# A token table beside the row buffers: when a mixture-of-experts kernel may load a row buffer anew

## The chip, the cores and the metric

The kernel runs on one core of a Trainium2 chip. The metric is the device time of one execution in microseconds (us); less is better. Quoted times are medians over several executions of one kernel. The profile is of one further execution.

## The reference

The reference is one transformer layer on 2048 tokens of 128 floats, in float32. First comes layer norm and a 16-head linear attention (cosformer) with its residual. Then comes layer norm and a mixture of experts (MoE) with its residual, which is the part that matters here:

```python
logits = xf @ gate_w                                   # 2048 x 8 experts
top_w, top_idx = jax.lax.top_k(logits, 2)
top_w = softmax(top_w)
h = gelu(einsum('td,edf->tef', xf, w1) + b1)           # 128 -> 512
y = einsum('tef,efd->ted', h, w2) + b2                 # 512 -> 128
out = einsum('ted,te->td', y, combine)                 # weights of the two chosen experts
```

## The kernel before

**Attention.** The tokens go through in four super-chunks of 512 (NS = 4). Each super-chunk's layer norm, gate logits, two best experts and row places are worked out while the next one's attention runs; the last one is handled in two halves (units 3 and 4).

**Sorting by expert.** For each token and each of its two experts GpSimd writes a row to `ybuf` in HBM with an indirect DMA (`rows_out`, L473). A row has 144 floats: the 128 normalised values, then the token's number in column D (as an unsigned integer; it names the row of `zbuf` to which the result goes), then the expert's weight in column D + 1. `ybuf` thus holds, expert by expert, blocks of 128 rows. NB = 39 blocks are computed; a table `tab` says for each block its expert and its place. The first 17 blocks (`FIRST[1]`) are listed before the last super-chunk has been sorted, the other 22 after a second table.

**A block's life.** For block b the steps are, engine by engine:

- SyncE, `load_block(b)`: reads the place from `tab`, issues the DMA of the block's 128 rows into row buffer `yb[b % 10]` (L376, 72 KB), and the DMA of the expert's first weights into `w1b[b % 6]` (L379, 256 KB). It runs ahead of the compute as far as the rings allow. Before the second DMA it waits until TensorE is through with block b - 6 (`h_ps`, L378). Before the first one, from block 10 on, it waits for `z_out` of block b - 10 (L373), that is, until that block's results have landed in HBM.
- TensorE, in the order written out in `step(b)`: transposes block b + 2 (`block_rows`, L1324), multiplies block b + 1 by w1 (`hidden`, L1337), multiplies block b by w2 (`down`, L1352). A transposition waits for the rows of its block (`yb_in`) and for `xb_ok`, the copy of the block before.
- ScalarE, `hidden(b)`: four activations (Gelu with bias, L638).
- VectorE: `block_rows(b)` loads the expert's number, copies the bias (L970) and copies the transposed block out of PSUM (L981); `weighed(b)` adds b2 (L986), and multiplies by the weight in column D + 1 of the row buffer (L990), which raises `z_ok`. In its order `block_rows(b + 3)` follows `weighed(b)`, and `weighed(b + 1)` follows that.
- GpSimd, `results_out(b)`: an indirect DMA (L511) scatters the 128 result rows to `zbuf`. Its offsets are read from column D of the row buffer, so the row buffer is in use until then. The order is by hand: `RESULTS_AT` says which blocks are scattered once `z_ok` has come to 3, 4, 8, 9, ... 14, since GpSimd also has late `rows_out` to issue (`LATE_ROWS_AT`); from block 14 on each block is scattered once it is weighed.

`z` has eight buffers (ZR), the row buffers are ten (YR), w1's are six (WR). At the end SyncE and ScalarE wait for all scatters, load `zbuf`, VectorE adds it to the residual, and the output is stored.

In the trace the 39 blocks can be counted along a line: the first row of L990 is block 0; the first row of L1324 is block 2 and the first of L981 too (blocks 0 and 1 are turned and copied at L1252 and L976).

Of the kernel before, what the change touches and what calls it, by code (L numbers as in the profile page):

```python
# [25 lines left out]
U32 = mybir.dt.uint32  # L26
I32 = mybir.dt.int32

P = 128
T, D = 2048, 128  # L30
# [47 lines left out]
NB = (2 * T + E * (TB - 1)) // TB  # L78
# [19 lines left out]
YR, ZR, WR, XR = 10, 8, 6, 4  # L98

def moe_block(nc, x, Wq, bq, Wk, bk, Wv, bv, Wo, bo, gate_w, w1, b1, w2, b2,
              c_rot, c_pair, c_ident, c_small, c_tri, c_ids, out, ybuf, zbuf):
    with ExitStack() as ctx:
        def sb(name, shape, dt=F32):
            return ctx.enter_context(nc.sbuf_tensor(name, shape, dt))

        def sem(name):
            return ctx.enter_context(nc.semaphore(name))
# [66 lines left out]
        yb = [sb(f"yb{k}", [P, ROW]) for k in range(3)]  # L175
        w1b = [sb(f"w1b{k}", [P, F]) for k in range(2)]
        b1_all = sb("b1_all", [P, E, FB])
        b2_all = sb("b2_all", [P, E, D])
        b1t = sb("b1t", [P, XR, FB])
        zs = sb("zs", [P, 2, D])  # L180
        xb = sb("xb", [P, XR, P])
        acc = x_sb
# [33 lines left out]
        z_out = [sem(f"z_out{k}") for k in range(ZR)]  # L216
# [92 lines left out]
        z_ok = sem("z_ok")  # L309
# [8 lines left out]
        def _(sp):  # L318
# [52 lines left out]
            def load_block(b):  # L371

                if b >= YR:  # L373
                    sp.wait_ge(z_out[(b - YR) % ZR], 16 * ((b - YR) // ZR + 1))
                at = sp.value_load(tab[0:1, 1, b:b + 1], min_val=0, max_val=PLACES)
                sp.dma_start(yb[b % YR][:], ybuf[bass.ds(at, TB), :]).then_inc(yb_in[b % YR], 16)  # L376
                if b >= WR:
                    sp.wait_ge(h_ps, 2 * (b - WR) + 2)  # L378
                sp.dma_start(w1b[b % WR][:], w1[bass.ds(at // PITCH, 1), :, :].rearrange("e p n -> p (e n)")  # L379
                             ).then_inc(w1_in[b % WR], 16)  # L380
# [4 lines left out]
            for u in range(TABLES[0] + 1):  # L385
                unit_landed(u)
            sp.wait_ge(tab_ok, 1)
            load_block(0)
            load_block(1)
            sp.wait_ge(sc_ps, NS * PAIRS)  # L390
            for b in range(2, FIRST[1]):
                load_block(b)
# [16 lines left out]
        def _(pool):  # L409
# [98 lines left out]
            def results_out(b):  # L508
                if b >= PACED:
                    pool.wait_ge(z_ok, b + 1)  # L510
                pool.indirect_dma_start(zbuf, bass.IndirectOffsetOnAxis(ap=yb[b % YR][:, D:D + 1].bitcast(U32), axis=0),  # L511
                                        z[:, b % ZR, :], None, bounds_check=2 * T - 1, oob_is_err=False).then_inc(z_out[b % ZR], 16)

            for i in range(NS):
# [5 lines left out]
            for k in range(1, PACED + 1):  # L520
                pool.wait_ge(z_ok, k)
                for u, m in LATE_ROWS_AT.get(k, ()):
                    rows_out(u, m)
                for b in RESULTS_AT.get(k, ()):
                    results_out(b)
                if k == 2:
                    second_rows(NS)
            for b in range(PACED, NB):
                results_out(b)
# [135 lines left out]
        def _(dve):  # L665
# [291 lines left out]
            def row_of(all_experts, expert):  # L957
                return all_experts[:, bass.ds(expert, 1), :].rearrange("p e n -> p (e n)")

            def expert_of(b):  # L960

                if b == 0:
                    dve.wait_ge(tab_ok, 1)
                    dve.wait_ge(b_in, 32)
                if b == FIRST[1]:
                    dve.wait_ge(tab_ok, 2)
                which[b] = dve.value_load(tab[0:1, 0, b:b + 1], min_val=0, max_val=E - 1)
                if b >= XR:
                    dve.wait_ge(h_ok, (b - XR + 1) * FB)
                dve.tensor_copy(b1t[:, b % XR, :], row_of(b1_all, which[b]))  # L970

            def first_rows():
                expert_of(0)
                expert_of(1)
                dve.wait_ge(xT_ps, NS + 1)
                dve.tensor_copy(xb[:, 0:2, :], ps[:, 6, 0:2 * P].rearrange("p (b r) -> p b r", b=2)).then_inc(xb_ok, 2)  # L976

            def block_rows(b):
                expert_of(b)
                dve.wait_ge(xb_ps, b - 1)  # L980
                dve.tensor_copy(xb[:, b % XR, :], ps[:, 5, b % 2 * P:b % 2 * P + P]).then_inc(xb_ok, 1)  # L981

            def weighed(b):

                dve.wait_ge(z_ps, b + 1)
                dve.tensor_tensor(zs[:, b % 2, :], ps[:, z_bank(b), 0:D], row_of(b2_all, which[b]), ALU.add).then_inc(zs_ok, 1)  # L986
                if b >= ZR:
                    dve.wait_ge(z_out[b % ZR], 16 * (b // ZR))
                dve.wait_ge(zs_ok, b + 1)
                dve.tensor_scalar(z[:, b % ZR, :], zs[:, b % 2, :], yb[b % YR][:, D + 1:D + 2], None, ALU.mult  # L990
                                  ).then_inc(z_ok, 1)

            def add_results(k):
# [5 lines left out]
                dve.tensor_tensor(tile, tile, zin[:, 1, k * SC:(k + 1) * SC, :], ALU.add).then_inc(out_ok, 1)  # L999

            first_rows()
            taken(NS - 1, GROUPS - 2)
            taken(NS - 1, GROUPS - 1)
            residual(NS - 1, SC - 2)
            best_two(NS - 1, 5)
            block_rows(2)
            norm2_stats(NS)
            norm2(NS)
            places(NS - 1)
            shares(NS - 1)  # L1010
            weighed(0)
            normed2(NS)
            block_rows(3)
            weighed(1)
            block_rows(4)
            weighed(2)
            block_rows(5)
# [438 lines left out]
```

## Time and profile before

| | |
|---|---|
| median of 3 executions | 378.92 us (378.6 to 380.24) |
| the profiled execution, first to last instruction | 389.7 us; no other time is given for it |
| TensorE busy | 358.1 us, 92% |
| VectorE, ScalarE, GpSimd busy | 62%, 40%, 33% |
| MoE blocks in the trace | about 266 us (first row load) to 374 us (last scatter issued) |

The span is that of the execution under the profiler and lies 10.8 us above the median of the runs without it. Busy is the time in which an engine has an instruction running. A row of a timeline gives start, duration, engine, line and operation, what is written and read, a count where instructions of a kind are merged, and in brackets how long the engine was idle before and what ended that. The duration of a DMA-issuing row (SPq) is that of the issue and not of the transfer.

### The profile page before, as it was taken

Reading aid. Unit: us, or ns where it says so; the run is one execution under the profiler, and the core shown is the slowest. Engines: PE = TensorE matmul, PEld = TensorE weight load, DVE = VectorE, ACT = ScalarE, POOL = GpSimd, SP = SyncE. Lnnn points to the kernel's source line nnn. Section 1 sums busy time; section 2 is a strip of 40 time slices with the busy share of each in tenths; the row PEclk is TensorE's granted clock in tenths of the full one; section 3 lists DMA queues with packets and bytes.
Section 4 is the critical chain, followed back from the end, with each engine's and each line's share of the span. In section 5 each row is a group of like instructions: output and inputs, shape, how many; then the busy total and the mean of one; then the engine's idle time right before and its main releaser. Section 6 shows DMA issues by size and latency. Waiting matters only on the chain.

```text
span 389.7 us, 10955 instructions
## 1 busy us (share of the span) xinstructions
PE 358.1 (92%) x4125; PEld 323.4 (83%) x4125; DVE 241.4 (62%) x735; ACT 156.7 (40%) x369; POOL 129.8 (33%) x130
## 2 busy tenths in 40 slices
PE   8999999999999999999999999999978887999910
PEld 7777999888988988898998889898978777999910
DVE  4889664778756477875647787766545424444415
ACT  3773322565122256512225651222443434555500
POOL 4022511121285112028511302443265454444420
PEclk9999999999999999999999999999998989999985
DMA  7932432330001000000100007004625256876229
GB/s 252 332 156 84 177 130 96 156 129 2 16 31 33 16 2 1 0 19 31 41 8 3 0 14 219 24 19 115 179 93 144 81 166 179 234 203 188 63 81 248
DMA packets 32771, 38.64 MB, mean 99 GB/s; under 512 B 4139, under 2 KB 25024, under 8 KB 31696
## 3 DMA queue, kind: packets, MB, share of 16 engines
q1 hardware_dynamic: 27248, 31.90, 26.4%
q0 software_dynamic: 2272, 4.46, 3.3%
q10 hardware_dynamic: 3200, 1.58, 1.5%
q8 instruction: 34, 0.56, 0.6%
q14 instruction: 17, 0.14, 0.1%
HBM read 22.91 MB, written 15.47 MB: 98 GB/s over the span
## 4 chain that ended last, share of the span: by engine, by line
PE 79%; DVE 7%; DMA 4%; issue 4%; POOL 2%; another core or an unknown queue 1%; ACT 1%; DVEq 1%; SPq 1%; ACTq 0%; POOLq 0%
PE ps L1166 8%; PE ps L1352 8%; PE ps L1128 8%; PE ps L1173 7%; PE ps L1337 7%; PE ps L1145 7%; PE ps L1202 7%; PE ps L1047 5%; PE ps L1049 5%; PE ps L1048 5%; PE ps L1193 4%; PE ps L1092 3%; DMA zin<-zbuf 2%; PE ps L1297 2%; PE ps L1324 1%
## 5 line engine op out<-in xcount | busy, mean ns | idle before, releaser
L597 ACT ACTIVATE os<-ps 128x260 f32<-128x260 f32 x64 | 24.8, 388 | 103.4 <-PE ps L1173 103.3
L638 ACT ACTIVATE hT<-ps,b1t 128x128 f32<-128x128 f32 x156 | 44.9, 368 | 47.9 <-PE ps L1337 26.7
L473 POOL DMA_INDIRECT ybuf<-yr,slot x32 | 31.8, 994 | 75.3 <-DVE yr L845 32.8
L431 POOL TENSOR_TENSOR on<-tcs,rden 128x1024 f32<-128x1024 f32 x16 | 30.4, 1901 | 64.4 <-DVE rden L773 64.4
L511 POOL DMA_INDIRECT zbuf<-z,yb x39 | 37.9, 972 | 39.0 <-DVE z L990 22.3
L760 DVE TENSOR_TENSOR state<-ps,state 128x260 f32<-128x260 f32 x64 | 27.3, 427 | 35.5 <-ACT os L597 29.3
L1352 PE MATMUL ps<-w_sb,hT 128*128 x312 | 43.4, 284 | 3.5 <-DVE zs L986 3.3
L750 DVE TENSOR_TENSOR am<-ps,pair 128x1024 f32<-128x1024 f32 x32 | 38.7, 1208 | 10.0 <-issue 7.5
L1337 PE MATMUL ps<-xb,w1b 128*128 128x128 f32 x312 | 43.9, 286 | 0.0
L1352 PEld LDWEIGHTS ps<-w_sb,hT 128*128 128x128 f32 x312 | 39.3, 198 | 4.3 <-issue 4.2
L1166 PE MATMUL ps<-vcs,am 128*64 128x65 f32 x1024 | 42.5, 225 | 0.2 <-issue 0.2
L1166 PEld LDWEIGHTS ps<-vcs,am 128*64 128x64 f32 x1024 | 36.8, 137 | 3.9
L1337 PEld LDWEIGHTS ps<-xb,w1b 128*128 128x128 f32 x312 | 39.7, 199 | 0.0
L1173 PE MATMUL ps<-vcs,kn 128*64 128x130 f32 x512 | 39.6, 275 | 0.0
L1128 PE MATMUL ps<-qT,kT 64*128 64x128 f32 x512 | 38.0, 285 | 1.0 <-DVE am L750 0.9
L1128 PEld LDWEIGHTS ps<-qT,kT 64*128 64x128 f32 x512 | 31.7, 187 | 7.3 <-issue 6.6
L1145 PE MATMUL ps<-state,qT 64*128 64x130 f32 x480 | 34.8, 279 | 0.5 <-DVE tcs L766 0.4
L715 DVE TENSOR_SCALAR vcs<-os,cs 128x512 f32<-128x512 f32 x64 | 32.6, 551 | 1.1
L1145 PEld LDWEIGHTS ps<-state,qT 64*128 64x128 f32 x480 | 30.2, 187 | 2.5 <-DVE tcs L766 1.4
L1202 PE MATMUL ps<-wo_sb,oT 128*128 128x128 f32 x256 | 31.6, 278 | 0.0
L1202 PEld LDWEIGHTS ps<-wo_sb,oT 128*128 128x128 f32 x256 | 29.8, 192 | 1.7 <-issue 1.4
L711 DVE TENSOR_TENSOR os<-ps,bv_all 128x512 f32<-128x512 f32 x32 | 22.0, 689 | 14.7 <-PE ps L1049 14.7
(120 smaller groups left out, 585.7 us busy)
## 6 DMA issues: line engine op xcount, KB each, us to landing
w1b<-in_L_ffn_w SPq DMA_DIRECT2D x39, 256.0 KB
ybuf<-blank SPq DMA_DIRECT2D x8, 1152.0 KB, 4.7
yb<-ybuf SPq DMA_DIRECT2D x39, 72.0 KB
w_sb<-in_L_ffn_w SPq DMA_DIRECT2D x8, 256.0 KB
x_sb<-in_L_attn_x SPq DMA_DIRECT2D x4, 256.0 KB, 5.4
pair<-c_pair SPq DMA_DIRECT2D x16, 64.0 KB, 2.4
zin<-zbuf SPq DMA_DIRECT2D x4, 256.0 KB, 5.5
zin<-zbuf ACTq DMA_DIRECT2D x4, 256.0 KB, 6.0
```

The source lines that it names most:

```text
L473: pool.indirect_dma_start(ybuf, bass.IndirectOffsetOnAxis(ap=slot[:, k, c:c + 1], axis=0), yr[:, k, c, :], None).then_inc(y_out[u], 16)
L511: pool.indirect_dma_start(zbuf, bass.IndirectOffsetOnAxis(ap=yb[b % YR][:, D:D + 1].bitcast(U32), axis=0), z[:, b % ZR, :], None, bounds_c ...
L638: act.activation(hT[:, b % 2, f, :], ps[:, b % 2 * 2 + f // 2, f % 2 * P:f % 2 * P + P], ACT.Gelu, bias=b1t[:, b % XR, f:f + 1]).then_inc( ...
L715: last = dve.tensor_scalar(vcs[:, m // 2, (m % 2) * 8:(m % 2) * 8 + 8, s, 0:DH], vb[:, m % 2, :].rearrange("p (h d) -> p h d", d=DH), cs4[ ...
L750: dve.tensor_tensor(am[:, p % 2, :, :, :], ps[:, 0:2, :].rearrange("p r (q t) -> p r q t", t=P), pair[:, c, None, None, :].broadcast_to([P ...
L1128: last = mm(ps[:, r, b * P:(b + 1) * P], kT[rows, of, c * P:(c + 1) * P], qT[rows, of, c * P:(c + 1) * P], start=True, stop=True)
L1145: mm(ps[:, 2 + 2 * (n % 2) + r, 0:2 * CS].rearrange("p (s b v) -> p b s v", s=2, b=2)[:, q, :, :], qT[rows, 2 * g + q, c * P:(c + 1) * P], ...
L1166: mm(ps[t:t + 64, 2 + 2 * (n % 2) + r, q * VW:q * VW + VW], am[:, n // 2 % 2, r, (2 * g + q) % (PH // 2), t:t + 64], vcs[:, c, g * GH + 2 ...
L1173: last = mm(ps[64 * r:64 * r + 64, 2 + 2 * (n % 2) + q, 2 * CS:3 * CS], kn[:, c, (2 * g + q) * P + r * DH:(2 * g + q) * P + (r + 1) * DH], ...
L1202: last = mm(ps[:, 7, at:at + D], oT[:, c % 2, pr, :], wo_sb[:, pr, :], start=(pr == 0), stop=(pr == NP - 1))
L1337: last = mm(ps[:, b % 2 * 2 + f // 2, f % 2 * P:f % 2 * P + P], w1b[b % WR][:, f * P:(f + 1) * P], xb[:, b % XR, :], start=True, stop=True ...
L1352: last = mm(ps[:, z_bank(b), 0:D], hT[:, b % 2, f, :], w, start=(f == 0), stop=(f == FB - 1))
```

## The change

A table `tokens` of 128 x 39 integers is added. In `block_rows(b)`, after the copy of the transposed block, VectorE copies column D of the row buffer to column b of the table; for blocks 0 and 1 it does so ahead of their common copy in `first_rows`. The scatter of block b reads its offsets from the table. `load_block(b)` now waits, from block 10 on, until block b - 10 is weighed (`z_ok`) and no longer until its scatter has landed.

```diff
+        tokens = sb("tokens", [P, NB], U32)
...
             def load_block(b):
 
                 if b >= YR:
-                    sp.wait_ge(z_out[(b - YR) % ZR], 16 * ((b - YR) // ZR + 1))
+                    sp.wait_ge(z_ok, b - YR + 1)
...
             def results_out(b):
                 if b >= PACED:
                     pool.wait_ge(z_ok, b + 1)
-                pool.indirect_dma_start(zbuf, bass.IndirectOffsetOnAxis(ap=yb[b % YR][:, D:D + 1].bitcast(U32), axis=0),
+                pool.indirect_dma_start(zbuf, bass.IndirectOffsetOnAxis(ap=tokens[:, b:b + 1], axis=0),
                                         z[:, b % ZR, :], None, bounds_check=2 * T - 1, oob_is_err=False).then_inc(z_out[b % ZR], 16)
...
+            def tokens_of(b):
+                dve.tensor_copy(tokens[:, b:b + 1], yb[b % YR][:, D:D + 1].bitcast(U32))
+
             def first_rows():
                 expert_of(0)
                 expert_of(1)
                 dve.wait_ge(xT_ps, NS + 1)
+                tokens_of(0)
+                tokens_of(1)
                 dve.tensor_copy(xb[:, 0:2, :], ps[:, 6, 0:2 * P].rearrange("p (b r) -> p b r", b=2)).then_inc(xb_ok, 2)
 
             def block_rows(b):
                 expert_of(b)
                 dve.wait_ge(xb_ps, b - 1)
                 dve.tensor_copy(xb[:, b % XR, :], ps[:, 5, b % 2 * P:b % 2 * P + P]).then_inc(xb_ok, 1)
+                tokens_of(b)
```

## Rows read from the trace of the kernel before

**Rows 1.** Busy time, granted clock and DMA share in three stretches of the MoE.

```profile
core 0: us, PE busy (x) PEld busy (x) DVE busy (x) ACT busy (x) POOL busy (x), PEclk, DMA share, GB/s
286.00:304.00 18.00, 14.27 (x108) 13.54 (x108) 7.99 (x45) 7.07 (x25) 9.83 (x12) 0.91 0.39 116
304.00:330.00 26.00, 20.63 (x161) 19.82 (x160) 9.12 (x40) 10.39 (x36) 12.64 (x13) 0.93 0.52 150
330.00:368.00 38.00, 37.94 (x326) 37.06 (x325) 17.94 (x76) 21.74 (x77) 18.43 (x19) 1.00 0.64 179
```

**Rows 2.** Waits of TensorE from 303 to 370 us, the only row.

```profile
PE ps L1324 <- DVE xb L981: 5.4, 4, 1.9
```

**Rows 3.** Waits in SyncE's queue after 255 us: in total, times, longest.

```profile
SPq L375 <- DMA zbuf<-z,yb: 3.3, 5, 1.2
SPq L379 <- PE ps L1337: 3.2, 2, 2.4
```

**Rows 4.** SyncE's loads: block 9's weights, blocks 10, 12, 13.

```profile
287.95 0.33 SPq L379 DMA_DIRECT2D w1b<-in_L_ffn_w  x1
294.56 0.33 SPq L376 DMA_DIRECT2D yb<-ybuf  x1
...
296.79 0.33 SPq L379 DMA_DIRECT2D w1b<-in_L_ffn_w  x1
299.58 0.01 SPq L376 DMA_DIRECT2D yb<-ybuf  x1
...
308.18 0.51 SPq L376 DMA_DIRECT2D yb<-ybuf  x1
308.74 0.71 SPq L379 DMA_DIRECT2D w1b<-in_L_ffn_w  x1
```

**Rows 5.** TensorE around the transposition of block 13 (311.38).

```profile
307.68 0.30 PE L1324 MATMUL ps<-ident,yb 128*128 128x128 f32 x1
...
311.38 0.30 PE L1324 MATMUL ps<-ident,yb 128*128 128x128 f32 x1 [1.40 <-DVE xb L981]
...
313.36 0.27 PE L1324 MATMUL ps<-ident,yb 128*128 128x128 f32 x1
```

**Rows 6.** VectorE: block 7 weighed, then block 9, and the copy of 12.

```profile
304.10 0.29 DVE L990 TENSOR_SCALAR z<-zs,yb 128x128 f32<-128x128 f32 x1
...
309.69 0.29 DVE L986 TENSOR_TENSOR zs<-ps,b_all 128x128 f32<-128x128 f32 x1 [2.17 <-remote]
...
310.94 0.29 DVE L981 COPY xb<-ps 128x128 f32<-128x128 f32 x1
```

**Rows 7.** GpSimd's scatters, two of a burst of three, and the next.

```profile
306.47 0.98 POOL L511 DMA_INDIRECT zbuf<-z,yb  x1 [0.30 <-issue]
307.75 0.97 POOL L511 DMA_INDIRECT zbuf<-z,yb  x1 [0.31 <-issue]
311.15 0.97 POOL L511 DMA_INDIRECT zbuf<-z,yb  x1 [2.43 <-DVE z L990]
```

**Rows 8.** DMA issues by kind on the page: KB, median us from issue to landing.

```profile
pair<-c_pair SPq DMA_DIRECT2D x16, 64.0 KB, 2.4
zin<-zbuf SPq DMA_DIRECT2D x4, 256.0 KB, 5.5
```

**Rows 9.** All engines in the steady part: block 22 weighed, blocks 26 and 27 turned.

```profile
341.63 0.29 DVE L990 TENSOR_SCALAR z<-zs,yb 128x128 f32<-128x128 f32 x1
...
343.00 0.27 PE L1324 MATMUL ps<-ident,yb 128*128 128x128 f32 x1
...
344.98 0.30 PE L1324 MATMUL ps<-ident,yb 128*128 128x128 f32 x1
```

**Rows 10.** VectorE by form from 330 to 370 us.

```profile
L986 DVE TENSOR_TENSOR zs<-ps,b_all 128x128 f32<-128x128 f32 x20 | 5.8, 291 | 9.4 <-issue 6.9 <-PE ps L1352 2.6
L970 DVE COPY b1t<-b_all 128x4 f32 x20 | 3.4, 170 | 9.4 <-ACT hT L638 8.6 <-issue 0.8
```

**Rows 11.** All z and L511 instructions: duration in ns, least, median, most.

```profile
L990 DVE TENSOR_SCALAR z<-zs,yb x39: 285/286/565, 283.6 to 372.8; 128x128 f32<-128x128 f32 x39
L511 POOL DMA_INDIRECT zbuf<-z,yb x39: 969/970/998, 291.6 to 373.9; - x39
```

**Rows 12.** VectorE's last copy of a block, near the end.

```profile
368.50 0.28 DVE L981 COPY xb<-ps 128x128 f32<-128x128 f32 x1
```

**Rows 13.** The common copy of blocks 0 and 1, and TensorE's first `hidden`.

```profile
270.64 0.42 DVE L976 COPY xb<-ps 128x256 f32<-128x256 f32 x1
...
275.33 1.06 PE L1337 MATMUL ps<-xb,w1b 128*128 128x128 f32 x8
```

## The prediction

> **What bounds the kernel now.** I read the stretches first, then who waits, then single timelines. From 330 to 368 us TensorE is busy 37.94 of 38 us at full clock [rows 1]: a block costs 1.98 us there (343.00 to 344.98, [rows 9]), and nothing that arrives earlier can shorten it. From 304 to 330 us it is busy only 20.63 of 26 us, and from 286 to 304 us 14.27 of 18 us [rows 1]. Those 5.4 and 3.7 us are the only places where a change in load order can gain, so the question is what these gaps wait for.
>
> TensorE's waits name VectorE's copy of the block before (5.4 us, four times) and no DMA at all [rows 2]. The transposition of block 13 shows it. It starts at 311.38, right after the copy of block 12 at 310.94 + 0.29 = 311.23 [rows 5, 6]. That copy is late because `weighed(9)` began only at 309.69 after 2.17 us of idleness, released by something the profile can't name ("remote", [rows 6]). In the same time GpSimd issues scatters back to back, at 306.47 and 307.75, with 0.3 us between them [rows 7], and VectorE goes on some 1.9 us after the last of a burst has started. The later gaps have the same look: a burst of three scatters, then VectorE's late row. So what I see is a chain from GpSimd's bursts to late signals to VectorE to TensorE. The change leaves the order of the scatters, `RESULTS_AT`, as it is.
>
> **What the removed wait costs today.** SyncE does stand still. Block 9's weights are issued at 287.95 and block 10's rows at 294.56; block 12's rows go at 299.58, block 13's at 308.18 [rows 4]. Block 13 needs the landing of block 3's scatter, which by `RESULTS_AT` isn't issued until block 7 is weighed. The row of waits at that line books 3.3 us in five waits [rows 3], much less than the 8.6 us from 299.58 to 308.18; it keeps only what it can match, so I go by the timeline.
>
> Does it reach TensorE? A load of 64 KB by SyncE lands in 2.4 us [rows 8]; the 72 KB of block 13 then land at 308.18 + 2.4 = 310.6, and TensorE turned the block at 311.38. Slack 0.8 us. The weights, issued at 308.74, are used 2.1 us after that, about 313.5. The trace has no landing time for them; the bounds are 2.4 us as for 64 KB and 5.5 us as for 256 KB from HBM [rows 8], giving 311.1 to 314.2. The row that names TensorE's waits has no DMA [rows 2], so I take them as in time. In this profiled execution the removed wait is thus hidden behind the late copy, and taking it away alone is worth 0.
>
> **The same without the profiler.** The profiled span, 389.7 us, is 10.8 us over the median of 378.92. The gaps of the MoE sum to 5.4 + 3.7 = 9.1 us, of the same size, so I reckon that part of them does not exist in a timed run. Then the loads have less cover. In the steady part a block is turned 5.3 us after the weighing of the block six before it (block 22 is weighed at 341.63, block 27 turned at 344.98, block 28 hence at 344.98 + 1.98 = 346.96, [rows 9]). Block 7 is weighed at 304.10 [rows 6], so an undisturbed TensorE would turn block 13 at 309.4, while its rows land at 310.6. The delay is 1.1 us. It is paid once: block 14 follows by SyncE's pace of one load in 1.7 us (block 13's rows at 308.18, and its weights 0.56 later, then 1.1 us to the next), faster than TensorE's 1.98. So the gain lies between 0 (all gaps are real in timed runs) and 1.1 us (none is). I take the middle, 0.5 us: 378.9 - 0.5 = 378.4.
>
> **What the loads do instead.** After the change SyncE is held by `h_ps` alone, the wait for block b - 6 at the weights. Block 12's rows could go at 296.79 + 1.1 = 297.9, block 13's 1.7 us later at 299.6, some 8.6 us earlier than now. Behind the new wait on `z_ok` the same things queue as before (place, rows, weights), and `z_ok` is raised before the scatter is issued, so the wait can never end later than the old one. From block 17 on loads also need the second table and the late rows, which have not changed; the order can gain up to 8 us of lead and no more, and in the steady part the lead is of no use [rows 1]. The same bytes move, a part of them from the 304 to 330 stretch (DMA share 0.52) to the one before (0.39) [rows 1]. There they meet the late rows of units 3 and 4. I cost that at 0.
>
> **The added copies.** There are 39 copies of 128x1. None is in the trace; the nearest row is the 128x4 copy from SBUF to SBUF, 170 ns, 20 of them [rows 10]. The lower bound is the pace of overlapped rows, near 0.1 us; the upper one is 0.17 us of VectorE each, 6.6 us in all. They stand between the copy of a block and L986 of an earlier block, and ahead of L986 VectorE idles 9.4 us in 20 blocks, 0.47 us each [rows 10]. That covers 0.17 us with 0.3 us to spare, so they cost 0. In the stage with gaps they stand before an idle time of some 2 us [rows 6]. The two in `first_rows` stand in front of the common copy of blocks 0 and 1 at 270.64; TensorE's first use of it is at 275.33, 4.3 us after its end [rows 13]. No copy stands behind the last block's: VectorE's last one starts at 368.50 [rows 12], and the three scatters that end the stage follow later. Were the cover gone, 39 x 0.17 = 6.6 us would be the price.
>
> The scatter's offsets come from another place in SBUF, the same 128 numbers; L511 keeps its 970 ns [rows 11].
>
> A rule speaks against such copies. L511 takes 969 to 998 ns in all 39 cases although L990, SBUF to SBUF too, runs beside some of them [rows 11]; only L990 itself is sometimes long, up to 565 ns. The Trainium skill (SBUF — State Buffer, "SBUF: two separate sides") says that VectorE in a mode using two ports and GpSimd lock each other out of a shared port for a whole instruction, and that fp32 copies within SBUF hold up GpSimd's descriptor writing. By that rule each copy would delay a scatter by its own length, 0.17 us, off the path, or wait for one. The trace agrees only in so far as L990 is at times long.
>
> **The rivals.**
>
> *A, more than 1.1 us is gained (0.16).* Weights too may be late today: at 5.5 us they land at 314.2, against an undisturbed need at 309.4 + 2.1 = 311.5, which is 2.7 us. Or the gaps themselves come from the crowd of catching-up loads and scatters in 304 to 330, and go when loads are spread: half of the 5.4 us gives 2.7 as well. Time 378.9 - 2.7 = 376.2. For it: the gaps end at 330, about when SyncE has caught up. Against: TensorE waits for no DMA [rows 2], and at 286 to 304 there are gaps of the same look while SyncE is standing still [rows 1, 4].
>
> *B, slower: copies outgrow their cover (0.07).* A copy that has to wait for GpSimd to finish a scatter (970 ns, [rows 11]) may take as long as the worst L990 beyond its usual, 565 - 286 = 279 ns, on top of its 170: 450 ns against 470 of cover. With the full 970 ns before it a copy takes 1.14 us, 0.67 beyond cover; of the 20 blocks in the filled stretch half may meet a scatter: 0.67 x 10 = 6.7 us, 385.6 at worst. At half that strength it is 3.3 us, 382.2. It decides from 0.47 us of copy on. Against it: L970, the same kind of copy, has a mean of 170 ns in the same stretch [rows 10].
>
> *C, nothing at all (within the forecast, but 0.0 us).* All gaps are real without a profiler: 378.9.
>
> A fourth, that earlier loads crowd out the late rows and delay the second table's blocks (0.05), bites where a late row lands after block 16's load is issued and holds the queue at block 17; I put it at one landing of 64 KB less the lead that the blocks have now, 2.4 - 0.8 = 1.6 us [rows 8], 380.5.
>
> **How the numbers follow.** The forecast with C holds 0.72, and the range of this case alone is 377.6 to 379.6 with the scatter of the timed runs. A has 0.16, B 0.07, the fourth 0.05. A change under 0.5%, 1.9 us, can't be told from none here; the bounds are 377.0 and 380.8. Faster: A, and a little of the forecast's low end, 0.19. Slower: B and a bit of the fourth, 0.09. The range reaches to A's 376.2 and stops at 380.3, short of B.
>
> **What would show it.** Right: SyncE's rows of block 13 go out near 300 instead of 308.18; TensorE's gaps between 286 and 330 stay, with VectorE's "remote" idleness after scatter bursts, and from 330 on a block costs 1.98 us; the new copy takes 0.1 to 0.2 us, and the idleness ahead of L986 shrinks by about that. Wrong: TensorE's busy time in the stretch from 304 to 330 rises well above 20.63 us (A), or idle TensorE appears after 330 with VectorE named as releaser (B). A timed gain above 2 us with an unchanged pattern of gaps would mean that the loads mattered in a way that this profile hides.

## The result, and the profile after

| | before | changed |
|---|---|---|
| median | 379.85 us (8 runs, 378.6 to 380.4 but for one of 406.98) | 376.93 us (375.08 to 378.09, 8 runs) |
| ratio, 95% interval | | 0.9921, 0.9898 to 0.9943 |
| profiled execution: span, own time | 389.7 us, not known | 375.2 us, 377.03 us |

The change saves 0.8% of 379.85, about 3.0 us (2.2 to 3.9 by the interval); the execution of 406.98 us counts as slow and is left out of the ratio. The forecast was 378.4 us, with 376.2 to 380.3 as its range. The time lies inside the range but below what the likeliest case allowed (377.6), and the chance given to a gain over 0.5% was 0.19.

After the change a profiled execution's own time is known: it is its span plus 1.8 us (377.03 - 375.2). So a profile doesn't stretch this kernel, and the first profile of the kernel before, 10.8 us above the median, was of an odd execution; why it was slow isn't known. A new profile of the same program (experiment e1) has a span of 377.7 us and a time of 379.58. Both sides are read from these two from here on. The columns are those of [rows 1].

The kernel before, profiled anew:

```profile
286.00:304.00 18.00, 16.92 (x142) 15.80 (x141) 9.83 (x47) 9.20 (x32) 11.88 (x14) 1.00 0.46 128
304.00:330.00 26.00, 24.50 (x204) 23.45 (x204) 11.40 (x48) 13.59 (x48) 13.55 (x15) 1.00 0.76 220
```

The changed kernel:

```profile
286.00:304.00 18.00, 17.01 (x146) 16.29 (x144) 10.61 (x60) 9.35 (x34) 12.07 (x14) 1.00 0.68 195
304.00:330.00 26.00, 25.68 (x214) 24.67 (x213) 12.69 (x63) 13.81 (x49) 14.76 (x16) 1.00 0.70 199
```

Of the 9.1 us of gaps in [rows 1] only 1.1 + 1.5 = 2.6 us are in a usual execution of the old kernel, at full clock throughout; after the change 1.0 + 0.3 = 1.3 are left. The waits say which went. From 284 to 356 us, in total, times, longest; first the old kernel, then the changed one:

```profile
PE ps L1324 <- DMA yb<-ybuf: 1.5, 2, 1.1
PE ps L1324 <- DVE xb L981: 0.9, 2, 0.7
```

```profile
PE ps L1331 <- DVE xb L987: 0.9, 2, 0.6
PE ps L1359 <- DVE zs L993: 0.2, 1, 0.2
```

The first row is new beside [rows 2]: TensorE did wait for row buffers. The timeline of the old kernel shows where. SyncE issues the rows of blocks 12, 13, 14 and 15:

```profile
292.85 0.33 SPq L376 DMA_DIRECT2D yb<-ybuf  x1
...
299.94 0.33 SPq L376 DMA_DIRECT2D yb<-ybuf  x1
...
301.75 0.33 SPq L376 DMA_DIRECT2D yb<-ybuf  x1
...
303.41 0.33 SPq L376 DMA_DIRECT2D yb<-ybuf  x1
```

TensorE turns blocks 13, 14, 15 and 16:

```profile
301.86 0.33 PE L1324 MATMUL ps<-ident,yb 128*128 128x128 f32 x1
...
305.12 0.33 PE L1324 MATMUL ps<-ident,yb 128*128 128x128 f32 x1 [1.15 <-DMA yb<-ybuf]
...
307.75 0.33 PE L1324 MATMUL ps<-ident,yb 128*128 128x128 f32 x1 [0.34 <-DMA yb<-ybuf]
...
309.71 0.27 PE L1324 MATMUL ps<-ident,yb 128*128 128x128 f32 x1
```

Block 13 is turned 1.92 us after its rows were issued (299.94 to 301.86), with no wait booked, so these rows landed within 1.92 us. Block 14's took 3.37 us from issue to transposition and block 15's 4.34, and TensorE stood waiting for both. In the four other profiles with the old wait and ten buffers (e2, e5, e6, e11, below) it is the same: block 13 is turned 1.86 to 1.91 us after its issue, block 14 only 2.8 to 3.2 us after, with a booked wait of 0.6 to 1.0 us. After the change the same four transpositions of blocks 13 to 16 follow at a pace of 2.0 to 2.1 us with nothing in brackets, and the rows of block 13 were issued at 291.48, 10.6 us ahead:

```profile
302.12 0.27 PE L1331 MATMUL ps<-ident,yb 128*128 128x128 f32 x1
...
304.11 0.30 PE L1331 MATMUL ps<-ident,yb 128*128 128x128 f32 x1
...
306.25 0.27 PE L1331 MATMUL ps<-ident,yb 128*128 128x128 f32 x1
...
308.24 0.30 PE L1331 MATMUL ps<-ident,yb 128*128 128x128 f32 x1
```

The second place is the end, where nothing was expected. The page's rows of the final load, KB each and median us to landing; old kernel, then the changed one:

```profile
zin<-zbuf SPq DMA_DIRECT2D x4, 256.0 KB, 5.6
zin<-zbuf ACTq DMA_DIRECT2D x4, 256.0 KB, 6.1
```

```profile
zin<-zbuf SPq DMA_DIRECT2D x4, 256.0 KB, 4.8
zin<-zbuf ACTq DMA_DIRECT2D x4, 256.0 KB, 5.3
```

The last scatter is issued at 361.81 in the one and at 360.49 in the other, so from there to the end it is 377.7 - 361.81 = 15.9 us and 375.2 - 360.49 = 14.7 us:

```profile
361.81 0.97 POOL L511 DMA_INDIRECT zbuf<-z,yb  x1 [0.31 <-issue]
```

```profile
360.49 0.97 POOL L512 DMA_INDIRECT zbuf<-z,tokens  x1 [0.34 <-issue]
```

In the chain of work that ended last (start, duration), the scatter's landing takes 2.08 us in both, and the final load differs by 1.19 us:

```profile
361.81 2.08 DMA zbuf<-z,yb
365.66 7.90 DMA zin<-zbuf
```

```profile
360.49 2.08 DMA zbuf<-z,tokens
364.35 6.71 DMA zin<-zbuf
```

The two spans differ by 2.5 us. From the transposition of block 12 to that of block 18 it is 14.3 us (299.43 to 313.74) against 12.7 (300.00 to 312.66), which is 1.65; the end gives 1.2; the rest, 0.35 us the other way, is spread over the other stretches. So there are two terms, a known one that was sized too small, and one that the forecast didn't have.

The added copy is within what was costed (durations as minimum, median and maximum in ns). The scatters have the median of e1, 972 ns; their longest is 1027 ns against 1003 in e1:

```profile
L974 DVE COPY tokens<-yb x39: 140/144/154, 267.1 to 355.4; 128x1 uint32<-128x1 uint32 x39
L512 POOL DMA_INDIRECT zbuf<-z,tokens x39: 970/972/1027, 286.7 to 360.5; - x39
```

### The profile page after: what moved, and what is told of

Same layout as the page of the kernel before. It is cut to its first block, busy times and chain, and to the rows that moved or that the text cites. A ratio compares the mean times of both kernels' runs of the same rounds, so it can differ in the third digit from the quotient of the medians.

```text
span 375.2 us, 10993 instructions
## 1 busy us (share of the span) xinstructions
PE 351.7 (94%) x4125; PEld 319.0 (85%) x4125; DVE 244.9 (65%) x774; ACT 156.5 (42%) x369; POOL 130.1 (35%) x130
## 4 chain that ended last, share of the span: by engine, by line
PE 82%; DVE 5%; DMA 5%; issue 3%; POOL 1%; ACT 1%; SPq 1%; ACTq 0%; DVEq 0%; POOLq 0%
PE ps L1135 9%; PE ps L1173 9%; PE ps L1359 8%; PE ps L1344 8%; PE ps L1152 7%; PE ps L1180 7%; PE ps L1209 7%; PE ps L1054 6%; PE ps L1056 5%; PE ps L1055 5%; PE ps L1200 4%; PE ps L1099 3%; DMA zin<-zbuf 2%; PE ps L1331 1%; DMA ident<-c_ident 1%
## 5 line engine op out<-in xcount | busy, mean ns | idle before, releaser
L512 POOL DMA_INDIRECT zbuf<-z,tokens x39 | 38.0, 975 | 31.1 <-DVE z L997 25.6
L1344 PE MATMUL ps<-xb,w1b 128*128 128x128 f32 x312 | 42.3, 278 | 0.0
L1359 PEld LDWEIGHTS ps<-w_sb,hT 128*128 128x128 f32 x312 | 37.8, 191 | 1.9 <-issue 1.4
L1135 PE MATMUL ps<-qT,kT 64*128 64x128 f32 x512 | 37.2, 284 | 1.0 <-DVE am L751 0.9
L1344 PEld LDWEIGHTS ps<-xb,w1b 128*128 128x128 f32 x312 | 37.9, 192 | 0.0
L1152 PE MATMUL ps<-state,qT 64*128 64x130 f32 x480 | 33.3, 277 | 0.0
```

Of the source, the lines that this page charges most:

```text
L512: pool.indirect_dma_start(zbuf, bass.IndirectOffsetOnAxis(ap=tokens[:, b:b + 1], axis=0), z[:, b % ZR, :], None, bounds_check=2 * T - 1, o ...
L1135: last = mm(ps[:, r, b * P:(b + 1) * P], kT[rows, of, c * P:(c + 1) * P], qT[rows, of, c * P:(c + 1) * P], start=True, stop=True)
L1152: mm(ps[:, 2 + 2 * (n % 2) + r, 0:2 * CS].rearrange("p (s b v) -> p b s v", s=2, b=2)[:, q, :, :], qT[rows, 2 * g + q, c * P:(c + 1) * P], ...
L1344: last = mm(ps[:, b % 2 * 2 + f // 2, f % 2 * P:f % 2 * P + P], w1b[b % WR][:, f * P:(f + 1) * P], xb[:, b % XR, :], start=True, stop=True ...
L1359: last = mm(ps[:, z_bank(b), 0:D], hT[:, b % 2, f, :], w, start=(f == 0), stop=(f == FB - 1))
```

## The experiments

Three theories stood against each other. G (called L in the last runs): rows come late at one place, behind the scatter of block 3 that is held back until block 7 is weighed, and this is paid once. K: the gaps of the first profile are usual, and spreading the loads dissolves them. P, formed after the first four runs: the new table moves other tiles in SBUF (the on-chip memory, 128 partitions), and their new places make DMAs faster. All ratios are to the kernel before on the same chip, with 95% intervals.

**e1, the kernel before once more.** No edit.

> The kernel before, unchanged, profiled anew. Theory G (the gaps of TensorE between 286 and 330 us in the first profile are not in usual executions, and the gain is made of late loads): a new profile has a span near 378 us and few gaps, TensorE waits at the transposition of block 13 for its rows by 1 to 3 us, about the size of the gain. Theory K (gaps are usual, earlier loads dissolve them): a new profile again has 5 us or more of gaps spread over 286 to 330 us. The time against before is 1.00 within 0.3% by either.

Measured: 379.62 us, ratio 0.9995 (0.9980 to 1.0011), span 377.7. Clearly G: few gaps, no low clock, and waits for rows at blocks 14 and 15 (above), although not at block 13. GpSimd issues its scatters in bursts of three here too, 0.3 us apart:

```profile
296.93 0.99 POOL L511 DMA_INDIRECT zbuf<-z,yb  x1 [1.45 <-DVE z L990]
298.22 0.98 POOL L511 DMA_INDIRECT zbuf<-z,yb  x1 [0.30 <-issue]
299.50 0.97 POOL L511 DMA_INDIRECT zbuf<-z,yb  x1 [0.30 <-issue]
```

and VectorE's longest wait ahead of L986 from 284 to 330 us is 1.8 us, by TensorE, none by "remote". The chain from bursts to late signals that the forecast read in [rows 6, 7] thus isn't a property of this kernel's usual runs.

**e2, the copies with the old wait.**

```diff
-                    sp.wait_ge(z_ok, b - YR + 1)
+                    sp.wait_ge(z_out[(b - YR) % ZR], 16 * ((b - YR) // ZR + 1))
```

> The changed kernel with SyncE's old wait: the table is filled and the scatters read it, but a row buffer is still loaded anew only once its block's scatter has landed. Theory G and theory K: the copies are covered, so the time is that of before, ratio 0.998 to 1.002. Rival (the gain comes from the scatters' new offsets or from the shape of VectorE's order): 0.992 as for the full change.

Measured: 378.12 us, ratio 0.9976 (0.9953 to 0.9999). That lies just below what G and K allow for what should do nothing, and is 0.9 us. TensorE still waits 1.2 us for rows, and blocks 12 to 18 take 14.3 us as before, but the final load has 5.0 and 5.4 us. This gave rise to theory P.

**e3, 16 row buffers in the kernel before.**

```diff
-YR, ZR, WR, XR = 10, 8, 6, 4
+YR, ZR, WR, XR = 16, 8, 6, 4
```

> The kernel before with 16 row buffers in place of 10 and nothing else: no copies, the old wait, but block 13 doesn't wait for block 3's scatter (blocks 0 to 15 have no row buffer wait at all). Theories G and K, by which only the moment of the loads counts: the whole gain, ratio 0.990 to 0.994. If the copies or offsets gave the gain: 1.00.

Measured: 377.61 us, ratio 0.9954 (0.9936 to 0.9971), 1.7 us gained. The moment of the loads is worth a gain without any copy or new wait, but not the whole. Blocks 12 to 18 take 12.2 us, TensorE waits for no rows, and the final load stays at 5.6 and 6.1 us: the first of the two terms alone.

**e4, the new wait for blocks 13 to 17 only.**

```diff
+                    if 13 <= b <= 17:
                         sp.wait_ge(z_ok, b - YR + 1)
+                    else:
+                        sp.wait_ge(z_out[(b - YR) % ZR], 16 * ((b - YR) // ZR + 1))
```

> The changed kernel, but only blocks 13 to 17 wait for the weighing; all others wait for the landed scatter as before. Theory G (one delay at the blocks behind the held scatter of block 3, paid once): the whole gain, 0.990 to 0.994. Theory K or a gain in the steady part, block by block: less than half of the gain, 0.996 to 1.00.

Measured: 377.52 us, ratio 0.9939 (0.9917 to 0.9962), with blocks 12 to 18 in 12.3 us. This contains the gain of the table's place too, since the table stands where it does in the full change; against e2, which has the same places and the old wait for all blocks, five blocks of 29 bring 1.4 of 2.1 us, and the interval overlaps the full change's. Its profiled execution has the shortest span, 374.2 us, with that of e8. Against K.

**e5 and e6, an unused tile in the kernel before.** The change moves `zin`, w2 and four of the six w1 buffers by 160 bytes in each partition. That `zin` starts 96 bytes past a multiple of 256 before the change, and at a multiple of 256 after it, was read from the compiled programs; no run kept here shows the addresses themselves, only what each shift does. The unused tile has 160 bytes in e5 and 32 in e6, where those tiles start 128 past a multiple.

```diff
+        pad = sb("pad", [P, 40])
         zs = sb("zs", [P, 2, D])
```

In e6 it is `[P, 8]`.

> The kernel before with an unused tile of 160 bytes in each partition where the change puts its table: no copies, no new wait, only the tiles behind it (w2, four of six w1 buffers, zin, z) move as in the changed kernel, zin and the weights to a start that is a multiple of 256 bytes. Theory P (the last microsecond of the gain is the place of zin and the weights in SBUF): the final load of zbuf takes 4.8 to 5.4 us in place of 5.6 to 6.1, the stretch from the last scatter's landing to the end is 12.7 us and not 13.8, and the ratio is 0.996 to 0.998. If the table's use gives it: 1.00 and 13.8 us.

Measured: 377.38 us, ratio 0.9948 (0.9927 to 0.9968), 15.9 down to 14.9 us from the last scatter to the end. The final load is as theory P expected; the ratio is below its 0.996 to 0.998, though the interval reaches into it. The final load in e5:

```profile
zin<-zbuf SPq DMA_DIRECT2D x4, 256.0 KB, 4.8
zin<-zbuf ACTq DMA_DIRECT2D x4, 256.0 KB, 5.4
```

> The kernel before with an unused tile of 32 bytes at the same place: zin and the weights start at an odd multiple of 128 bytes. Theory P with 256 bytes as the step that counts: nothing of the gain, ratio 1.00, final load 5.6 us. With 64 or 128 bytes as the step: 0.997, final load 4.9 us. Before, they start 96 bytes past a multiple of 256.

Measured: 378.96 us, ratio 0.9996 (0.9977 to 1.0014); from the last scatter to the end 15.7 us. The final load in e6:

```profile
zin<-zbuf SPq DMA_DIRECT2D x4, 256.0 KB, 5.4
zin<-zbuf ACTq DMA_DIRECT2D x4, 256.0 KB, 5.9
```

Of the steps considered, 64, 128 and 256 bytes, theory P holds with 256 only: an empty tile gives 0.5%, and one of another size gives nothing that can be told from noise. The median of e5 is about 2.0 us below that of before, and the end explains 1.0 of them. Blocks 12 to 18 took 13.4 us there against 14.3, but 13.5 in e6 too, which is no faster on the clock; where the rest of e5 is, or whether it is there at all (the interval is 1.2 to 2.8 us), stays open. So does the difference to e2, which has the same places and the copies besides and gained 0.9 us; their intervals overlap, and e10 speaks against a price of the copies.

**e7, the table behind all other tiles.** The full change, with `tokens` allocated after `z`, so that nothing else moves.

```diff
-        tokens = sb("tokens", [P, NB], U32)
...
         z = sb("z", [P, ZR, D])
+        tokens = sb("tokens", [P, NB], U32)
```

> The changed kernel with its table allocated behind all other tiles, so that no other tile moves from its place of before. Theory P: the loads are early but the place is the old one: end stretch 13.8 us, ratio 0.994 to 0.996. If the place is of no account: 0.992 as for the full change.

Measured: 378.51 us, ratio 0.9970 (0.9954 to 0.9985), and 16.1 us from the last scatter to the end (378.5 - 362.37). Without the accident of its place the change is worth 0.3%. It fell a little short of what was expected by P, 0.994 to 0.996; the product of e5 and e7, 0.9948 x 0.9970 = 0.9918, is close to the full change's 0.9921.

**e8, more tiles at multiples of 256 bytes.** The full change with the table last and four unused tiles, so that x, all w1 buffers and z start at such places too.

```diff
+        pad0 = sb("pad0", [P, 32])
         x_sb = sb("x_sb", [P, NC, D])
...
+        pad1 = sb("pad1", [P, 56])
         yb = [sb(f"yb{k}", [P, ROW]) for k in range(3)]
...
+        pad2 = sb("pad2", [P, 16])
         zs = sb("zs", [P, 2, D])
...
+        pad3 = sb("pad3", [P, 16])
         z = sb("z", [P, ZR, D])
+        tokens = sb("tokens", [P, NB], U32)
```

> The changed kernel with four unused tiles so that x, all w1 buffers, w2, zin and z start at a multiple of 256 bytes. Theory P: at least as fast as the changed kernel, perhaps 0.3 to 0.8 us faster (loads of x, the final stores from x, two more w1 buffers): ratio 0.989 to 0.992. Otherwise 0.992.

Measured: 376.56 us, ratio 0.9934 (0.9909 to 0.9959). The ratio is above the 0.989 to 0.992 that was expected, and its interval includes the full change's 0.9921: no further gain can be seen. That the other loads are hidden behind work, and only the final one lies open, fits this but isn't shown by itself.

**e9, e3 and e5 together.** 16 row buffers and the 160 unused bytes in the kernel before.

> The kernel before with 16 row buffers (e3) and the unused 160 bytes (e5): early loads and the better places, but no table, no copies and the old wait. If the two terms add, and the copies are free: the ratio of the full change, 0.989 to 0.993. If the copies or the new wait have a price of their own: up to 1 us below the full change, 0.987 to 0.990.

Measured: 376.03 us, ratio 0.9918 (0.9892 to 0.9944). Two sizes, and no line of the change, give what the change gives.

**e10, five copies in place of one.**

```diff
             def tokens_of(b):
                 dve.tensor_copy(tokens[:, b:b + 1], yb[b % YR][:, D:D + 1].bitcast(U32))
+                for k in range(4):
+                    dve.tensor_copy(spare[:, k, b:b + 1], yb[b % YR][:, D:D + 1].bitcast(U32))
```

> The changed kernel with five copies of each block's token column in place of one (four of them into a spare tile behind all others). A copy takes 143 ns, and VectorE idles 0.45 us ahead of L993 in the filled stretch. If one copy is covered with room to spare: five of them, issued about 0.1 us apart, just about fit, and the time is that of the full change, 0.992, or up to 1 us above it. If already the first copy is paid for: four more cost at least 4 x 0.1 x 39 = 15 us, ratio over 1.02.

Measured: 376.91 us, ratio 0.9936 (0.9913 to 0.9959). VectorE by form from 330 to 352 us: busy, mean ns, then the idle time before. The changed kernel:

```profile
L993 DVE TENSOR_TENSOR zs<-ps,b_all 128x128 f32<-128x128 f32 x11 | 3.2, 292 | 5.0 <-PE ps L1359 4.3 <-issue 0.5
```

With five copies:

```profile
L977 DVE COPY spare<-yb 128x1 uint32<-128x1 uint32 x44 | 3.6, 143 | 0.0
L996 DVE TENSOR_TENSOR zs<-ps,b_all 128x128 f32<-128x128 f32 x11 | 3.2, 291 | 2.1 <-PE ps L1362 1.7 <-issue 0.3
```

44 more copies took 2.9 us of idle time, 0.066 us each, less than the 0.1 us that the forecast had as its lower bound. Four more of them per block leave the time within the interval of the full change, so the one copy is covered, by several times its size.

**e11, the new wait from block 18 on only.** The reverse of e4 (`if b >= 18`).

> The changed kernel with the new wait from block 18 on alone; blocks 10 to 17 wait for the landed scatter. Theory L (the late loads of blocks 13 to 15 are the whole gain of the new wait): TensorE's blocks 12 to 18 take 13.4 to 14.3 us as before, and the ratio is that of the copies with the old wait, 0.996 to 0.999. If the steady part gains by earlier loads: below 0.995.

Measured: 377.82 us, ratio 0.9968 (0.9950 to 0.9985), blocks 12 to 18 in 13.9 us, still with a wait for rows (0.6 us). It is what the copies and the new places give in e2; no gain of the filled stretch from earlier loads can be seen.

**e12, nine row buffers in the kernel before.** The suspected delay, one block earlier.

```diff
-YR, ZR, WR, XR = 10, 8, 6, 4
+YR, ZR, WR, XR = 9, 8, 6, 4
```

> The kernel before with nine row buffers in place of ten: now block 12 waits for block 3's scatter, one block earlier. Theory L: TensorE stands still for block 12 by about one block more, 2 us, ratio 1.004 to 1.007. If the moment of the loads were hidden by other waits, as forecast: 1.00.

Measured: 381.62 us, ratio 1.0062 (1.0038 to 1.0086). Now it is block 12 that TensorE waits for, in full view:

```profile
302.65 0.33 PE L1324 MATMUL ps<-ident,yb 128*128 128x128 f32 x1 [2.37 <-DMA yb<-ybuf]
```

This transposition comes 1.95 us after the issue of its rows (300.70), as block 13's does with ten buffers. One buffer less costs 2.4 us, about one block (2.0 us), and six more save 1.7: the delay is real.

Over all profiles of these kernels the wait for rows (named "DMA yb<-ybuf") is 0.6 to 1.5 us where blocks 13 to 17 keep the old wait with ten buffers (e1, e2, e5, e6, e11), 3.2 us with nine, and absent where they load early (e3, e4, e7 to e10 and the changed kernel). From block 12 to block 18 the first five take 13.4 to 14.3 us, 13.9 on average; the seven that load early take 12.2 to 12.7, 12.5 on average. From the last scatter to the end the five where `zin` lies off a multiple of 256 bytes (e1, e3, e6, e7, e12) take 15.9 us on average and the eight where it lies at one 14.9. So by all profiles the two terms are 1.4 and 1.0 us, 2.4 together, inside the 2.2 to 3.9 of the timed runs.

## Why the prediction was right or wrong

**The range and the sign were right, the likeliest case was too small**: 0.5 us forecast, 3.0 measured. That the range holds 376.93 at all is luck: the likeliest case by itself ended at 377.6, and it was rival A that carried the bound down to 376.2, by causes that the runs don't bear out. Three steps made the difference.

*"In this profiled execution the removed wait is thus hidden behind the late copy."* True of that execution, but it was odd. In a usual one (e1) there is no late copy at block 13, and nothing hides the wait. The text did suspect this from 389.7 against 378.92, and its paragraph "The same without the profiler" put the wait at up to 1.1 us, which is right in kind. Its reason was wrong, though: the profiler adds nothing, as the 1.8 us between span and time show in every later profile.

*"The delay is 1.1 us. It is paid once".* The cause was right: the row buffer of block 13 waits for the scatter of block 3, held until block 7 is weighed, and from block 17 on no wait for rows is booked. Where it is paid was wrong. The forecast put all of it at block 13, by a landing of 2.4 us; that was too long, as block 13's rows land within 1.86 to 1.92 us in the five profiles with the old wait, and no wait is booked there. (From block 12 to block 13 TensorE takes 2.4 us in these five against 2.0 to 2.2 where loads are early, so up to 0.4 us may be lost there unbooked.) It then let block 14 go free, "by SyncE's pace of one load in 1.7 us". The pace is right (299.94, 301.75, 303.41 in e1), but it counts issues and not landings: block 14's rows are turned 2.8 to 3.4 us after their issue and TensorE waits 0.6 to 1.15 us for them, and in e1 0.34 more for block 15's. Why these land later than block 13's isn't shown; each of them follows on other row and weight loads in the queue. The stretch from block 12 to block 18 is 1.65 us shorter after the change in the pair read above, 1.4 on average over the profiles; in the timed runs the term is 1.1 us by e7 (0.6 to 1.7) and 1.7 by e3 (1.1 to 2.4). The forecast took half of its 1.1 us as well, because it couldn't tell which gaps were real.

*"The scatter's offsets come from another place in SBUF"* was all that was said of the table's place. That the table moves every tile behind it by 160 bytes was put at nothing without a word. This is the missing term. At the end of the kernel 1.0 us of it can be seen on average, 1.2 in the pair read above. In the timed runs it is 2.0 us by e5 (1.2 to 2.8), 0.9 by e2 (0.0 to 1.8) and 1.2 by e11 (0.6 to 1.9), the latter two with the copies and, for blocks 10 to 17, the old wait; which of the two terms is the larger isn't settled.

**The rivals.** A had the size (2.7 us, 376.2) and neither of its causes: no wait for weights appears, and the gaps of 9.1 us that it would dissolve aren't there in usual runs. Nearest to what happened is its crowd of catching-up loads, since the rows of blocks 14 and 15 do land late. The gain came as two terms of which the forecast had one. B, copies that outgrow their cover, did not come: 143 ns on average against the 170 taken, the longest 154, and a price of 0.066 us of idle time (e10). The fourth, late rows crowded out, did not come either; its place, block 17, is among the blocks that e4 loads early at a gain. C, nothing at all, is excluded by the interval.

**What went as forecast.** No load goes out later by the new wait: block 10's rows went out at 284.25 against 289.24 in e1, and block 13's at 291.48, even earlier than the 299.6 forecast, since block 10's no longer wait for block 0's scatter either. The filled stretch shows no gain (e11). The scatters keep the median of e1, 972 ns, and the longest copy takes 154 ns, so the rule of the Trainium skill on the shared port (SBUF — State Buffer, "SBUF: two separate sides") that the forecast weighed did not show itself: no copy waited for GpSimd, and a scatter longer by up to 0.02 us (1027 ns against 1003) is all that could be put down to it. **What did not:** the gaps between 286 and 330 us with their "remote" idleness, which were to stay, are not in usual executions.

## What to carry to other kernels

Before costing an edit against a profile, compare the profiled execution with the timed ones; where they differ by 3%, as here, the gaps in it may hide the very wait that the edit removes. The issue times of a queue that catches up say when loads start; when they land has to be read at each consumer. Count as part of an edit every tile that its new tile moves, and test that part by an empty tile of the same size: here it was about a third of the gain or more (1.0 us at the end alone, of 3.0), and without the wait's removal it could be had for nothing. Where a ring of buffers and an order written by hand meet, look for the one block whose release is held longest: one buffer less or six more tell its price at once.

## What the runs showed of the hardware

A load of rows (72 KB) landed within 2.0 us of its issue, when it came after a pause of the queue (block 13 in e1, e2, e5, e6 and e11: 1.86 to 1.92; block 12 in e12: 1.95). The next one, issued 1.8 us later with a load of weights in between, was turned 2.8 to 3.4 us after its issue, with TensorE waiting for it.

The filled stretch from block 18 to block 38 took 40.1 to 40.5 us in seven profiles and 41.0 to 41.3 in six others, without any edit that goes with it (the old kernel, the changed one, e7, e9, e10 and e12 are among the long ones, e2 to e6, e8 and e11 among the short). TensorE's listed waits don't tell the two kinds apart, and this 0.8 us is not explained.
